# Second dense attention: the dummy products between TensorE's score tiles are removed

## The reference, cut to what matters

```
        scores = jnp.einsum('bhqd,bhkd->bhqk', q, k) / scale
        scores = jax.nn.sigmoid(scores - mu) * jnp.exp(scores)
        scores = scores / jnp.sum(scores, axis=-1, keepdims=True)
        out = jnp.einsum('bhqk,bhkd->bhqd', scores, v)
```

## Time and profile before

| | |
|---|---|
| median of 3 runs | 4155.5 us (4150.63 to 4158.05) |
| the profiled execution's own time | 4152.44 us |
| its span, first to last instruction | 4150.6 us |
| TensorE busy in the span | 3473.8 us (84%) |
| VectorE, ScalarE busy | 2690.9 us (65%), 2596.3 us (63%) |
| mean granted clock in the span | 0.92 |
| the second dense attention's score tiles | 1211.7 to 2293.5 us |

### The profile page before, as it was taken

How to read it: one execution, slowest core, us unless ns; L and a number is a source line. 1 busy time by engine, 2 the same in 40 slices (tenths; PEclk the granted TensorE clock), 3 DMA queues, 4 the chain that set the end, 5 groups by cost and what they waited for, 6 DMA issues and landing times. The chain is left out here.

```text
span 4150.6 us, 54356 instructions
## 1 busy us (share of the span) xinstructions
PE 3473.8 (84%) x20444; PEld 1530.9 (37%) x20444; DVE 2690.9 (65%) x4473; ACT 2596.3 (63%) x4281; POOL 1360.0 (33%) x1266
## 2 busy tenths in 40 slices
PE   7995888889958898988888799879987899686776
PEld 4672122212221221222222366546655456332333
DVE  5225989989746656565555677557756523568887
ACT  2221676767858989989999587548754332325554
POOL 0501482010011000010000588358840261406886
PEclk9996999999979989999999899989988999897877
DMA  4111131111021001011000111111102012290001
GB/s 141 39 42 45 38 61 29 22 32 17 2 55 26 16 20 27 7 25 16 16 1 1 28 34 35 25 23 34 35 15 86 12 56 56 49 112 6 1 16 26
DMA packets 140860, 137.40 MB, mean 33 GB/s; under 512 B 42632, under 2 KB 105908, under 8 KB 140596
## 3 DMA queue, kind: packets, MB, share of 16 engines
q1 hardware_dynamic: 131060, 116.08, 12.7%
q0 software_dynamic: 8192, 16.79, 1.8%
q10 hardware_dynamic: 1344, 1.05, 0.1%
HBM read 64.12 MB, written 33.82 MB: 24 GB/s over the span
## 5 line engine op out<-in xcount | busy, mean ns | idle before, releaser
L476 PE MATMUL PS<-t 50*128 50x512 bf16 (+2 forms) x3072 | 737.5, 396 | 203.4 <-ACT t L629 55.3
L609 ACT ACTIVATE t<-PS 128x512 f32<-128x512 f32 x1024 | 532.7, 602 | 236.2 <-PE PS L476 235.5
L748 DVE TENSOR_TENSOR t<-t 128x1536 f32<-128x1536 f32 (+1 forms) x384 | 585.1, 1591 | 122.7 <-ACT t L629 70.0
L664 DVE TENSOR_REDUCE t<-PS 128x1 f32<-128x1024 f32 x512 | 600.9, 1215 | 50.7 <-PE PS L468 46.5
L550 PE MATMUL PS<-t 128*9 128x512 f32 x4096 | 550.2, 610 | 12.7 <-DVE t L748 12.3
L476 PEld LDWEIGHTS PS<-t 50*128 50x128 bf16 (+2 forms) x3072 | 158.3, 94 | 985.2 <-ACT t L629 276.9
L631 ACT ACTIVATE t<-PS 128x1536 f32<-128x1536 f32 (+1 forms) x384 | 477.9, 1310 | 54.0 <-PE PS L476 37.1
L629 ACT ACTIVATE t<-PS 128x1536 f32<-128x1536 f32 (+1 forms) x384 | 477.1, 1310 | 34.6 <-PE PS L476 19.4
L468 PE MATMUL PS<-t 48*128 48x512 bf16 x1024 | 342.1, 404 | 45.2 <-DVE t L664 24.7
L1845 POOL TENSOR_TENSOR t<-t 128x512 f32<-128x512 f32 x128 | 159.8, 1270 | 575.8 <-ACT t L1710 575.3
L524 PE MATMUL PS<-t 128*128 128x384 f32 x544 | 269.1, 579 | 0.0
(11 more groups left out here) (413 smaller groups left out, 6329.5 us busy)
## 6 DMA issues: line engine op xcount, KB each, us to landing
t<-scr SPq DMA_DIRECT2D x336, 64.0 KB
t<-t SPq DMA_DIRECT2D x128, 128.0 KB, 2.3
scr<-t SPq DMA_DIRECT2D x96, 128.0 KB, 1.8
t<-t SPq DMA_DIRECT2D x16, 512.0 KB, 13.0
scr<-t SPq DMA_DIRECT2D x2, 2560.0 KB
t<-scr SPq DMA_DIRECT2D x16, 320.0 KB, 3.7
scr<-t SPq DMA_DIRECT2D x16, 320.0 KB, 2.6
t<-scr SPq DMA_DIRECT2D x48, 48.0 KB
```

The costliest lines, as they stand in the source:

```text
L476: return e.op.matmul(PS[:, bk, :], Kx[p // 4 % 2][lo:lo + rows, j, kb * 128:kb * 128 + 128], Qx[p // 4 % 2][lo:lo + rows, j, hf * 512:hf * ...
L609: e.op.activation(P[x % 4][:, 2 * hf + side, :], PS[:, bank((what, p, k, side, hf)), :], ACT.Exp, scale=S8).then_inc(*PW.up((p, k, side, hf)))
L664: e.op.tensor_reduce(MX[p % 2][:, side, qc:qc + 1], PS[:, 2 * side:2 * side + 2, :].rearrange("p a n -> p (a n)"), AX, ALU.max).then_inc(* ...
L748: e.op.tensor_tensor(o, o, SGM[(12 * p + 3 * blk + ti) % 3][:, 0:nu, :], ALU.mult).then_inc(*DG.up((p, blk, ti)))
```

## The change

`fills` and its helper `taken` are deleted, and with them the three lines that issue a dummy ahead of a score tile. The order of all other work, the banks and the waits are as they were. The first attention never issued dummies.

```
-                def taken(p, k):
-
-                    if k < 0:
-                        p, k = p - 1, 7
-                    return p and k == 3 or any(True for _ in spread(p, k))
-
-                def fills(p, k, ti):
-
-
-                    return 2 <= k <= 4 and (ti == 2 or not taken(p, k - 1)) or (
-                        k == 5 and ti < 2 and not taken(p, 4))
-
...
                             bk = 3 * (n % 2)
                             n += 1
-                            if fills(p, 4 * ps + blk, ti):
-                                bm = take(e, ring.next(), ("fill", *i))
-                                e.op.matmul(PS[:, bm, 0:384], ident[:], XT[:, 0:384], start=True, stop=True)
                             take(e, bk, (what, *i), (AC if ps else PW, (what, *i)))
```

## The result

The changed kernel takes 4171.5 us (median of 8 runs) against 4152.53 for the kernel before (8 runs beside them). The ratio is 1.0040, interval 1.0026 to 1.0054: by the ratio 17 us slower. The forecast was +1.4 us and 4157, with the change taken for too small to be told from none (under 0.2%); the time lies in the forecast's range, and the change is twice those 0.2%.

A forecast was written before the change was run, and what follows sets the result against it. At full clock TensorE bounds neither half of a pair: ScalarE sets the first, VectorE the second. Terms of 0 + 1 + 1 - 0.6 = +1.4 us on 4152.4 gave 4153.8, forecast as 4157; range 4136 to 4188.

The forecast's parts named there:

- Term 4: Second halves of the second attention's pairs: half-clock PV costs 10.4 us, less 11 us paid now, -0.6 us.
- Terms 2 and 3: First halves of pairs: half-clock score tiles, +1 us; q/k products ending block 2 in six pairs, +1 us.
- Term 2: First halves of the second attention's pairs: score tiles alone at half clock, net +0.05 us a pair, taken as +1.
- Term 1: The 272 dummies themselves: 0.1 to 0.3 us in a pair's first half at full clock; counted as 0.
- (a): Second halves: clock returns one block later, PV at half clock; 4195, half of the pairs so 4175; chance 0.23.
- (b): Second attention: clock falls more rarely or returns earlier, VectorE never starved; -20 us, 4136; chance 0.21.
- (c): Second attention: half-clock time counts in full, TensorE being the bound throughout; 4370; chance 0.02.
- (d): Second attention: products gone, but clock and time do as before; 4155; chance 0.06.

The follow-up runs named there:

- e4_load2: Kernel before, with a second dummy ahead of the last tile of block 4, at the table load; ratio 0.9968, 4147.66 us against 4156.63.
- e6_load_only: Kernel before, with two dummies ahead of the last tile of block 4 and none anywhere else; ratio 1.0020, 4313.14 us against 4304.71.
- e5_short: Kernel before, with two 384-column dummies at the table load and all others cut to 192 columns; ratio 0.9949, 4282.3 us against 4304.71.
- e3_rows32: Kernel before, with all dummies kept but each using 32 rows of the identity instead of 128; ratio 1.0279, 4284.92 us against 4156.63.

## Why the prediction was right or wrong

**The time lies inside the range, but the change isn't the forecast's: +17 us, not +1.4. The step that failed is Term 4.** The second halves gave +20.7 us where I wrote -0.6. Term 4's sentence was "up to about 9.7 nothing is lost", worked out for VectorE alone. Two chains make the second half, and it lasts as long as the longer: VectorE's, 16.20, and ScalarE's, 14.78 busy plus its waits for tiles. ScalarE had only 16.20 - 14.78 = 1.42 us in hand. At half clock tiles (5,0) and (6,0) cost it 0.20 + 1.23 = 1.43, which I had noted as "in time" (for VectorE it was). From there each tenth of a microsecond counts, so the loss begins at t = 8.8, and the next wait is 1.34, not VectorE's 0.7 to 0.94.

The second half of the error is the return. I took a mean of 3.7 us behind PV 0; the 32 pairs show 2.8 to 6.2, mean 4.7. Worked out on the measured curve, my own eight delays would have given about 0.5 us a pair, 16 us instead of the 6.4 that I counted; the measured delays give about 29. So by this estimate the chain left out is worth some 10 and the late return some 13. Less the 11 us that before paid for the same thing (e4_load2 puts it at 12.7), 29 is 18 of the measured 20.7; the rest lies in the pairs with other products, for which I had +4. What sets the delay isn't settled: it repeats with the program (pairs 8 to 15 have 5.28, 5.88, 5.62, 5.95, 2.87, 4.30, 3.13 and 4.56 us, pairs 16 to 23 the same to 0.04), but no run here varied it by itself.

**What held.** The clock was at half in each of the 32 pairs: it stood there from the start of the first and fell in the other 31, 7.2 to 10.5 us in (one at 14.2), forecast 7.5 to 11; 0.73 over the stage, forecast 0.75; PV 0 at t = 5.96, forecast 5.8; tile (6,1) ready at 11.6, forecast 11.4. Terms 2 and 3 said +2 and the first halves gave -2.7. Score tiles at half clock cost as little there as I wrote: behind a second half of 16.20 us an ordinary first half lasts 16.50 in e6_load_only and 16.43 in before, +0.07 where Term 2 had +0.05. But the echo of the second half, which I didn't have, is larger. My sign for Term 2, first halves of 16.4 to 16.6 us, was missed by it: most ordinary ones last 16.25 to 16.43. Term 1 counted nothing for the dummies. e5_short shows what they cost where the clock stays up, about 0.2 us a first half, inside Term 1's 0.1 to 0.3; e3_rows32 shows them at half clock, 2 us a first half and more (18.3 to 20.4 us in ordinary pairs), which before seldom paid. My sign of being wrong, ordinary pairs a microsecond away from 32.7, was met by those of 33.8 us, like the one from 1308.4, and not by those of 32.5, like the one from 1342.2.

**The rivals.** (a) is nearest: "it decides as soon as the return lies beyond t = 10" came true in 24 of 32 pairs, and its price for half of them, 4175, is 3.5 us from the result (worked out as it is for all of them, half of 51 less 11, it would be 4170). Halves over 17.5 us were my sign for it, and they came. But its mechanism, VectorE starved, is the smaller of the two, by the 17.14 against 17.55 above. I had given it 0.23. (b): a return never too late; e4_load2 shows the size, -12.7 in the second halves, of which 9 were given back elsewhere. (c), half-clock time in full: the added time at half clock is 1099.9 x 0.54 - 1081.8 x 0.12 = 464 us, half of it 232, and 18 were lost. The Trainium skill's rule for the penalty ("TensorE: Matmul & The Clock Gate", Terms) would say the same 232; the trace doesn't agree, since ScalarE and VectorE bound the stage. (d): clock 0.73, refuted.

**A version that beats both** is e5_short: 0.5% faster than before, by the two ratios 0.9% faster than the changed kernel. The two weren't run on one chip.

## What to carry to other kernels

When a slower engine is hidden behind another, work out the slack of every engine that it feeds, not only of the one that ends last today: here ScalarE had 1.4 us in hand under VectorE, and that was used up before VectorE noticed. Work that only keeps a clock up is worth placing by the moment when the clock is needed (the table load ahead of the PV products) and cutting to the smallest size that holds it; score tiles alone at half clock were nearly free here, dummies at half clock ahead of them were not. And look at the next stretch too: a loss here shortened the one behind it, and a gain was partly lost again where a dummy had to wait for a bank and the clock fell.

## What the runs showed of the hardware

- With as many dummies of 384 columns, the stage's granted clock was 0.94 with 128 rows, 0.87 with 64 and 0.72 with 32; without any it was 0.73.
- With half of the columns (192 for 384) and a second dummy at the table load it was 0.97; with all columns and the second dummy 0.98.
- A 64-row fp32 product ran beside a score product in the other 64 partitions: 0.47 us from the dummy to the tile instead of 0.85. Where the tile began in the dummy's own partitions it was 0.95, and behind a 32-row dummy 0.84.
- The clock fell with TensorE never idle for long: in the stretch from 1342.3 that ends with a fall it was busy 6.29 of 7.90 us at 1.00, idle for 1.01 us at the longest. In the stretch from 1350.2 it was busy 11.84 of 17.00 us, with the clock at 0.50 throughout.
